# Window attention stage: one ring of 16 channel tiles for both statistics and normalisation, in a loop of 16 units per pass

## The reference, cut to what matters

```python
x = x + window_attention(group_norm(x, G=32), w_qkv, pos_emb, w_out, b_out)   # shifted 7x7 windows, 4 heads
t = x.reshape(B, H*W, C)
t = t + linear_attention(layer_norm(t), W, b)       # causal, with cumulative sums
t = t + recurrence(layer_norm(t), W, V, gamma, beta)

def _gn(v, G=32, eps=1e-5):
    g = v.reshape(B_, H_, W_, G, C_ // G)
    m = jnp.mean(g, axis=(1, 2, 4), keepdims=True)
    s = jnp.var(g, axis=(1, 2, 4), keepdims=True)
    return ((g - m) / jnp.sqrt(s + eps)).reshape(v.shape)
```

## Time and profile before

| | |
|---|---|
| median of 3 runs | 2037.19 us (2036.47 to 2037.60) |
| profiled execution | 2037.19 us |
| its span | 2035.6 us |
| PE, DVE, ACT, POOL busy | 95%, 82%, 72%, 63% |
| first stage | from 0 to about 804 us |
| mean DMA rate from 130 to 700 us | 139 GB/s |

### The profile page before, as it was taken

The page is one execution under the profiler, slowest core; times in us unless marked ns, Lnnn a source line. Parts: engine busy times, 40 slices in busy tenths (PEclk is TensorE's granted clock), DMA queues, the critical chain, the costliest instruction groups (busy, mean ns, idle before and its releaser), DMA issues. The chain is left out here.

```text
span 2035.6 us, 67390 instructions
## 1 busy us (share of the span) xinstructions
PE 1924.6 (95%) x20434; PEld 1673.7 (82%) x20434; DVE 1678.2 (82%) x5427; ACT 1466.1 (72%) x3774; POOL 1290.4 (63%) x1760
## 2 busy tenths in 40 slices
PE   3999999999999997899999999999999995699997
PEld 2888888888888886899999999999999993366664
DVE  6888888888888885799999999999999982255554
ACT  2777777777777775799999999999999971122221
POOL 2888888888888885444444444445444445577772
PEclk9999999999999999899999999999999996799998
DMA  5445454454445442122222222222222212466663
GB/s 152 143 136 145 132 146 139 139 140 138 141 137 146 133 111 75 38 61 63 59 61 61 59 63 59 61 61 59 63 59 60 62 48 61 109 195 202 185 208 113
DMA packets 246949, 214.80 MB, mean 106 GB/s; under 512 B 21312, under 2 KB 205984, under 8 KB 246880
## 3 DMA queue, kind: packets, MB, share of 16 engines
q1 hardware_dynamic: 246880, 213.92, 37.3%
HBM read 136.77 MB, written 77.07 MB: 105 GB/s over the span
## 5 line engine op out<-in xcount | busy, mean ns | idle before, releaser
L838 POOL TENSOR_SCALAR la_spread<-la_mv 112x4 f32<-112x4 f32 x231 | 54.6, 236 | 389.1 <-DVE la_mv L924 388.6
L544 POOL TENSOR_TENSOR wa_prob<-wa_prob,wa_peak 128x784 f32<-128x784 f32 x128 | 194.6, 1521 | 116.4 <-DVE wa_peak L433 116.3
L796 ACT ACTIVATE la_raised<-k_psum,la_bqk 128x224 f32<-128x224 f32 x448 | 200.5, 448 | 74.0 <-PE k_psum L690 74.0
L846 POOL TENSOR_TENSOR la_ln<-la_spread,k_exponent 112x4 f32<-112x4 f32 x231 | 239.5, 1037 | 0.3 <-POOL la_minus L839 0.3
L1282 ACT ACTIVATE main_y<-k_psum,sc_cols 128x448 f32<-128x448 f32 x112 | 70.9, 633 | 211.0 <-PE k_psum L1223 211.0
L690 PE MATMUL k_psum<-la_uT,la_wt 128*128 128x224 f32 x896 | 211.2, 358 | 0.0
L779 ACT ACTIVATE la_u<-la_xc,la_ln 112x128 f32<-112x128 f32 x448 | 201.0, 515 | 13.3 <-POOL la_ln L850 13.2
L813 ACT ACTIVATE la_u<-la_tn,la_ln 112x128 f32<-112x128 f32 x448 | 201.0, 515 | 10.1 <-POOL la_ln L850 10.1
L551 POOL TENSOR_TENSOR wa_prob<-wa_prob,wa_inv 128x784 f32<-128x784 f32 x128 | 195.0, 1523 | 10.2 <-DVE wa_inv L397 10.2
L797 ACT ACTIVATE la_positive<-k_psum,la_bqk 128x224 f32<-128x224 f32 x448 | 200.7, 448 | 0.0
L425 DVE TENSOR_TENSOR wa_prob<-k_psum,wa_bias 128x784 f32<-128x784 f32 x128 | 124.9, 976 | 78.3 <-PE k_psum L280 78.3
(11 more groups left out here) (147 smaller groups left out, 5883.3 us busy)
## 6 DMA issues: line engine op xcount, KB each, us to landing
wa_xw<-in_x_tok SPq DMA_DIRECT2D x128, 224.0 KB, 2.8
wa_xs<-in_x_cm SPq DMA_DIRECT2D x128, 196.0 KB, 2.5
wa_xT<-in_x_cm SPq DMA_DIRECT2D x128, 196.0 KB, 2.5
la_xc<-x SPq DMA_DIRECT2D x224, 112.0 KB, 2.0
t<-la_tn SPq DMA_DIRECT2D x224, 112.0 KB, 2.0
main_tb<-t SPq DMA_DIRECT2D x28, 896.0 KB, 6.0
out<-main_ob SPq DMA_DIRECT2D x28, 896.0 KB, 7.5
x<-wa_y SPq DMA_DIRECT2D x128, 112.0 KB
```

The lines of the kernel that those rows point to most:

```text
L544: nc.gpsimd.tensor_tensor(s, s, peak[:, k % S, :].unsqueeze(2).broadcast_to([128, PAIRS * HEADS, WIN]), ALU.subtract).then_inc(lowered, 1)
L796: nc.scalar.activation(raised[:, k, j, :], src, ACT.Exp, bias=bqk[:, j:j + 1])
L846: nc.gpsimd.tensor_tensor(rstd, spread[:, :], exponent[0:CH, 0:4], ALU.pow).then_inc(rooted, 1)
```

## The change

`xs` and its load go. `xT` becomes a ring of 16 slots (XS), loaded 15 units ahead (AHEAD), and both `measure` and `normalise` read it. POOL no longer waits for a load in `normalise`, since DVE's statistics of the same image have waited for it. The small buffers of the statistics (`stats`, `spread`, `grouped`, `variance`, `rstd`, `shift`) are doubled, one for even and one for odd images, and the waits that guarded a single one look one image further back. The slot of a ring of 16 and the parity of the image have to be known when the code is written, so the loop's body grows from 8 to 16 steps.

```diff
+        XS = 16
+        AHEAD = 15
-        xs = sb("xs", [128, S, ROWTOK])
-        xT = sb("xT", [128, S, ROWTOK])
-        stats = sb("stats", [128, NWR, 6])
-        rstd = sb("rstd", [128, 1])
+        xT = sb("xT", [128, XS, ROWTOK])
+        stats = sb("stats", [128, 2, NWR, 6])
+        rstd = sb("rstd", [128, 2, 1])
...
-        run = dict(first=-STATS - 3, last=NU + 6, lo=NWR, hi=NU - 2 * NWR, unroll=NWR)
+        run = dict(first=-AHEAD, last=NU + 6, lo=XS, hi=NU - XS, unroll=XS)
...
-                def load_for_statistics(n, k):
-                    if inside(n, NU):
-                        at_least(sp, measured, n - S + 1)
-                        sp.dma_start(xs[:, k % S], channels(n)).then_inc(s_loaded[k % S], 16)
-
                 def load_channels(n, k):
-                    if inside(n, NU):
-                        at_least(sp, normed, n - S + 1)
-                        sp.dma_start(xT[:, k % S], channels(n)).then_inc(x_loaded[k % S], 16)
+                    if not inside(n, NU):
+                        return
+                    at_least(sp, normed, n - XS + 1)
+                    sp.dma_start(xT[:, k % XS], x_cm[:, bass.ds(n, 1), :].rearrange("p o t -> p (o t)")).then_inc(x_loaded[k % XS], 16)
...
                 def step(n, k):
-                    load_for_statistics(n + STATS + 3, k + STATS + 3)
-                    load_channels(n + 3, k + 3)
+                    load_channels(n + AHEAD, k + AHEAD)
                     load_tokens(n + 2, k + 2)
                     store(n - 5, k - 5)
...
-                    dve.wait_ge(s_loaded[k % S], (n // S + 1) * 16)
-                    at_least(dve, aggregated, n // NWR)
-                    nc.vector.bn_stats(stats[:, k % NWR, :], xs[:, k % S, :]).then_inc(measured, 1)
+                    dve.wait_ge(x_loaded[k % XS], (n // XS + 1) * 16)
+                    at_least(dve, aggregated, (n - NWR) // NWR)
+                    nc.vector.bn_stats(stats[:, (k // NWR) % 2, k % NWR, :], xT[:, k % XS, :]).then_inc(measured, 1)
...
-                    at_least(pool, normed, n + 1)
-                    nc.gpsimd.tensor_tensor(rstd[:, :], variance[:, 1:2], exponent[:, 0:1], ALU.pow).then_inc(rooted, 1)
+                    at_least(pool, normed, n + 1 - NWR)
+                    nc.gpsimd.tensor_tensor(rstd[:, i, :], variance[:, i, 1:2], exponent[:, 0:1], ALU.pow).then_inc(rooted, 1)
...
                 def normalise(n, k):
-                    pool.wait_ge(x_loaded[k % S], (n // S + 1) * 16)
```

More of the change, by code:

```diff
@@ L112, in window_attention @@
         bias = sb("bias", [128, NWR, PAIRS, 2, WIN])
-        xs = sb("xs", [128, S, ROWTOK])
-        xT = sb("xT", [128, S, ROWTOK])
-        stats = sb("stats", [128, NWR, 6])
-        spread = sb("spread", [128, 3])
-        grouped = sb("grouped", [128, 3])
-        variance = sb("variance", [128, 2])
-        rstd = sb("rstd", [128, 1])
-        shift = sb("shift", [128, 1])
+        xT = sb("xT", [128, XS, ROWTOK])
+        stats = sb("stats", [128, 2, NWR, 6])
+        spread = sb("spread", [128, 2, 3])
+        grouped = sb("grouped", [128, 2, 3])
+        variance = sb("variance", [128, 2, 2])
+        rstd = sb("rstd", [128, 2, 1])
+        shift = sb("shift", [128, 2, 1])
         xn = sb("xn", [128, S, NWC, WPAD])
@@ L140, in window_attention @@
         bias_set, exponent_set = sem("wa_bias_set"), sem("wa_exponent_set")
-        s_loaded = [sem(f"wa_s_loaded{i}") for i in range(S)]
-        x_loaded = [sem(f"wa_x_loaded{i}") for i in range(S)]
+        x_loaded = [sem(f"wa_x_loaded{i}") for i in range(XS)]
         t_loaded = [sem(f"wa_t_loaded{i}") for i in range(S)]
@@ L184, in _ @@
             def _(sp):
-                def channels(n):
-                    return x_cm[:, bass.ds(n, 1), :].rearrange("p o t -> p (o t)")
-                def load_for_statistics(n, k):
-                    if inside(n, NU):
-                        at_least(sp, measured, n - S + 1)
-                        sp.dma_start(xs[:, k % S], channels(n)).then_inc(s_loaded[k % S], 16)
                 def load_channels(n, k):
-                    if inside(n, NU):
-                        at_least(sp, normed, n - S + 1)
-                        sp.dma_start(xT[:, k % S], channels(n)).then_inc(x_loaded[k % S], 16)
+                    if not inside(n, NU):
+                        return
+                    at_least(sp, normed, n - XS + 1)
+                    sp.dma_start(xT[:, k % XS], x_cm[:, bass.ds(n, 1), :].rearrange("p o t -> p (o t)")).then_inc(x_loaded[k % XS], 16)
                 def load_tokens(n, k):
@@ L240, in group_moments @@
                         return
-                    pe.wait_ge(spread_out, (n + 2) // NWR * 2 + 2)
+                    m = (n + 2) // NWR
+                    pe.wait_ge(spread_out, (m + 1) * 2)
                     if inside(n, NU):
                         pe.wait_ge(q_out, n + 1)
-                    nc.tensor.matmul(b_group, group[:, :], spread[:, :], start=True, stop=True).then_inc(group_ready, 1)
+                    nc.tensor.matmul(b_group, group[:, :], spread[:, ((k + 2) // NWR) % 2, :], start=True, stop=True).then_inc(group_ready, 1)
                 def queries(n, k):
@@ L363, in aggregate @@
                         return
-                    m = (n + 3) // NWR
-                    at_least(dve, group_ready, m)
+                    m, i = (n + 3) // NWR, ((k + 3) // NWR) % 2
+                    at_least(dve, group_ready, (n + 3 - NWR) // NWR)
                     dve.wait_ge(measured, (m + 1) * NWR)
                     apart(dve, dve_passed)
-                    nc.vector.bn_aggr(spread[:, 1:3], stats[:, :, :]).then_inc(aggregated, 1)
+                    nc.vector.bn_aggr(spread[:, i, 1:3], stats[:, i]).then_inc(aggregated, 1)
                     dve.wait_ge(aggregated, m + 1)
-                    nc.vector.tensor_scalar(spread[:, 0:1], spread[:, 1:2], -1.0, None, ALU.mult).then_inc(spread_out, 1)
-                    nc.vector.scalar_tensor_tensor(spread[:, 2:3], spread[:, 1:2], spread[:, 1:2], spread[:, 2:3],
+                    nc.vector.tensor_scalar(spread[:, i, 0:1], spread[:, i, 1:2], -1.0, None, ALU.mult).then_inc(spread_out, 1)
+                    nc.vector.scalar_tensor_tensor(spread[:, i, 2:3], spread[:, i, 1:2], spread[:, i, 1:2], spread[:, i, 2:3],
                                                    ALU.mult, ALU.add).then_inc(spread_out, 1)
@@ L377, in group_variance @@
                         return
-                    m = (n + 2) // NWR
+                    m, i = (n + 2) // NWR, ((k + 2) // NWR) % 2
                     dve.wait_ge(group_ready, m + 1)
-                    at_least(dve, shifted, m)
-                    nc.vector.tensor_copy(grouped[:, :], b_group).then_inc(group_out, 1)
+                    at_least(dve, shifted, (n + 2 - NWR) // NWR)
+                    nc.vector.tensor_copy(grouped[:, i, :], b_group).then_inc(group_out, 1)
                     dve.wait_ge(group_out, m + 1)
-                    nc.vector.scalar_tensor_tensor(variance[:, 0:1], grouped[:, 0:1], grouped[:, 1:2], grouped[:, 2:3],
+                    nc.vector.scalar_tensor_tensor(variance[:, i, 0:1], grouped[:, i, 0:1], grouped[:, i, 1:2], grouped[:, i, 2:3],
                                                    ALU.mult, ALU.add).then_inc(var_out, 1)
                     dve.wait_ge(var_out, m + 1)
-                    nc.vector.tensor_scalar(variance[:, 1:2], variance[:, 0:1], 0.0, GN_EPS, ALU.max, ALU.add).then_inc(var_kept, 1)
+                    nc.vector.tensor_scalar(variance[:, i, 1:2], variance[:, i, 0:1], 0.0, GN_EPS, ALU.max, ALU.add).then_inc(var_kept, 1)
                 def add_up(n, k):
@@ L520, in root @@
                         return
-                    m = (n + 1) // NWR
+                    m, i = (n + 1) // NWR, ((k + 1) // NWR) % 2
                     pool.wait_ge(var_kept, m + 1)
-                    at_least(pool, normed, n + 1)
-                    nc.gpsimd.tensor_tensor(rstd[:, :], variance[:, 1:2], exponent[:, 0:1], ALU.pow).then_inc(rooted, 1)
+                    at_least(pool, normed, n + 1 - NWR)
+                    nc.gpsimd.tensor_tensor(rstd[:, i, :], variance[:, i, 1:2], exponent[:, 0:1], ALU.pow).then_inc(rooted, 1)
                     pool.wait_ge(rooted, m + 1)
-                    nc.gpsimd.tensor_tensor(shift[:, :], grouped[:, 0:1], rstd[:, :], ALU.mult).then_inc(shifted, 1)
+                    nc.gpsimd.tensor_tensor(shift[:, i, :], grouped[:, i, 0:1], rstd[:, i, :], ALU.mult).then_inc(shifted, 1)
                     pool.wait_ge(shifted, m + 1)
@@ L536, in normalise @@
                     apart(pool, pool_passed)
-                    nc.gpsimd.tensor_scalar(xn[:, k % S, :, 0:WIN], xT[:, k % S, :].rearrange("p (w t) -> p w t", w=NWC),
-                                            rstd[:, :], shift[:, :], ALU.mult, ALU.add).then_inc(normed, 1)
+                    i = (k // NWR) % 2
```

(2 more changed lines are left out.)

## The result

| | time, us |
|---|---|
| before, median of 4 runs | 2036.83 (2034.84 to 2037.60) |
| changed, median of 4 runs | 2074.38 (2071.55 to 2075.21) |
| ratio | 1.0183, 95% interval 1.0166 to 1.0201 |

A forecast was written before the change was run, and what follows sets the result against it. The prediction took PE's own stream to bound the first stage's steady part (600.00 of 600 us filled). 2037.2 - 3.2 (start) + 17.5 (branches) + 5.2 (clock) = 2056.7, say 2056.5 us; range 2044 to 2072.

The forecast's parts named there:

- Start, -3.2 us: First stage's start: eight tiles in eight slots end waits of DVE and POOL, so PE's first matmul comes 3.2 us earlier.
- Nothing in the steady part for fewer loads, doubled buffers and later waits: First stage's steady beat: PE is full and no beat waits for DMA, so these edits change nothing.
- The body does not stay on chip; a branch back waits 3.5 us, five times: First stage's loop end: PE waits for the packet with the body's start, 5 x 3.5 = 17.5 us.
- the far branch: PE's branch at the program's very end, to code not yet brought: 3.93 us, used to price the branches back.
- The other engines miss as well: Rival, first stage's branches back: another engine also waits for its packet, up to 19.5 us added, 2076 us; chance 0.07.
- One pause per branch: First stage's five branches back: PE waits once at each, 3.5 us; no second pause in the sum.
- the branch lands just ahead of a packet's end: Rival, branches back: PE waits again for the next packet, five more waits of up to 3.5 us, 2074 us; chance 0.06.
- the main case: First stage's branches back: PE waits as priced, five times 3.5 us; chance 0.70.
- The clock, 1.05 us a branch: PE's clock may fall behind each branch's pause: 1.05 us lost each, bounds 0 and 2.1, 5.2 us in sum.

The follow-up runs named there:

- ring8_for_statistics: The kernel before with only the ring of the statistics' tiles given 8 slots, not 4, loop of 8 units kept; 2033.02 us, ratio 0.9981.
- before_body16: The kernel before with only the first stage's loop body enlarged from 8 to 16 units; 2079.55 us, ratio 1.0215.
- after_pad64: The changed kernel with 64 more instructions (semaphore increments) at the start of PE's stream, shifting its code; 2054.79 us.
- after_pad16: The changed kernel with 16 more instructions at the start of PE's stream, shifting its code; 2061.37 us.
- before_fill192: The kernel before with 192 more PE instructions in its loop body: 2086.54 us unmoved; the same body moved by 124 instructions: 2161.79 us.
- after_rotated: The changed kernel with PE's loop cut at another place of the step, order of instructions the same; 2053.67 us.

## Why the prediction was wrong

**Start, -3.2 us.** Right: the first matmul came 3.21 us earlier.

**Nothing in the steady part for fewer loads, doubled buffers and later waits.** Right: ring8_for_statistics keeps the second load and has the same gain, before_body16 has none of these edits and the whole loss.

**The body does not stay on chip; a branch back waits 3.5 us, five times.** Right in mechanism: five pauses of 3.4 to 3.6 us, 17.4 in sum against 17.5. That the size fits so closely is partly luck. The branches took 4.45 to 4.62 us, not the 3.93 of the far branch, but PE's matmuls of the keys ran until 1.2 us after the branch began, and I had counted as covered only the time until the next weight load was due (0.7 us). The two errors nearly cancel. The same pause was 3.0 us in after_pad64 and 3.9 in before_body16.

**The other engines miss as well** (a rival, 0.07). It did not happen: their instruction queue, q14, brought no packet between 216 and 700 us.

**One pause per branch.** This failed. The rival "the branch lands just ahead of a packet's end" had 0.06, and it is what happened, beside the main case and not in its place. The second pause was 1.6 us on average, 8.2 in sum (the rival had up to 3.5 each), at a spot that after_pad16 narrows to the body's first 16 instructions. I had written that nothing in the rows says where a body starts in its packet. The rows shown do not, but the trace of before could have bounded it: a packet is 16 KB, some 256 instructions, and q8's packets come at such distances of PE's stream, so their times and a count of PE's instructions give the place to some tens of instructions. I left that at a chance.

**The clock, 1.05 us a branch.** Too small by a factor of three, and above its upper bound of 2.1. What is left of 8.4 us after pauses of 3.5 and 1.6 is 3.3 us, and the granted clock of the five windows gives the same 16.3 us in sum. The clock fell at every branch, and it was down beyond the second pause: 0.51 and 0.52 from 219 to 226 us. With one pause, as in after_pad64, 4.7 less a pause of 3.0 is 1.7 us, nearer to the forecast and within its bounds. That kernel, which is the forecast's case of one pause, came out at 2054.8 us against the forecast 2056.5; after_pad16, also with one pause, at 2061.4, so this closeness is no proof of the sizes.

So the steps that failed are that PE waits only once at a branch back, and the size of the clock: the failing terms are the second pause (0 forecast, 8.2 us measured) and, in part through it, the clock (5.2 forecast, some 16 measured).

**The store's size** was taken from the Trainium skill ("Runtime: NRT & Kernel Launch", "Instruction fetch mechanics": 128 KiB on PE, which is eight packets of 16 KB). The pair before_fill192 bears it out. The same section also speaks of a window of two pages, outside of which a taken branch stalls, which the prediction did not say. Here that does not hold for PE: the kernel before goes back over seven packets, with no q8 packet from 130 to 700 us and branches of 0.21 us.

## What to carry to other kernels

A loop's body has a size limit on PE that no shape or buffer shows: eight packets of 16 KB with the one brought ahead, touched, not filled. (The other engines' limits were not reached here.) Count PE's instructions before doubling an unroll (here a transpose makes two, a weight load and a matmul, and an fp32 matmul four), and look whether the instruction queue is silent from the second pass on. Where a body must be larger, straight code was better than a loop here, since bringing code cost nothing and only branching back to it did; and where the gain wanted is a deeper ring at the start, give it a number of slots that fits the body as it is.

## What the runs showed of the hardware that I had not expected

- When the body is one packet too large, all its packets are brought again in each pass (nine of nine), though only one is too many.
- Some sixteen instructions past the edge, one kernel gave times from 2035 to 2092 us. A kernel as close to the edge as the one before can become up to 3% slower in some executions when PE code is added ahead of its loop; the cause of the spread is argued, not shown.
- PE's clock fell at all five pauses of 2.4 us in mean (after_rotated) and once held through 3.1 us (after_pad64, the third branch).
- A branch back to a missing packet left PE idle for 2.4 (after_rotated) to 3.9 us (before_body16) in mean, depending on where the code lay and, a little, on what was queued.
